# Recommendation tower, one core: a later place for layer 1, split index load at the head, low halves from copies in PSUM

## What is computed

```python
e = jnp.stack([tbl_0[ids[:, 0]], ..., tbl_25[ids[:, 25]]], axis=1)
combined = jnp.concatenate([e, r_dense_x[:, None, :]], axis=1)
z = jnp.einsum('bfd,bgd->bfg', combined, combined)[:, TRIU_I, TRIU_J]
h = jnp.concatenate([z, r_dense_x], axis=1)
h = jnp.maximum(h @ W_top1 + b_top1, 0.0)    # 479 x 512
h = jnp.maximum(h @ W_top2 + b_top2, 0.0)    # 512 x 256
y = h @ W_top3                               # 256 x 1
```

## Time and profile before

| what | value |
|---|---|
| time, median of 3 runs | 375.76 us (374.6 to 376.51) |
| profiled execution | 375.79 us, of it 373.8 us span |
| PE busy | 333.4 us (89%) |
| POOL busy | 252.8 us (68%), 256 gathers |
| DVE busy | 247.8 us (66%) |
| ACT busy | 203.4 us (54%) |
| granted TensorE clock, mean | 0.977 of 2.4 GHz |

### The profile page before, as it was taken

The page is one execution under the profiler, slowest core; times in us unless marked ns, Lnnn a source line. Parts: engine busy times, 40 slices in busy tenths (PEclk is TensorE's granted clock), DMA queues, the critical chain, the costliest instruction groups (busy, mean ns, idle before and its releaser), DMA issues.

```text
span 373.8 us, 9779 instructions
## 1 busy us (share of the span) xinstructions
PE 333.4 (89%) x4178; PEld 315.3 (84%) x4178; DVE 247.8 (66%) x298; ACT 203.4 (54%) x274; POOL 252.8 (68%) x262
## 2 busy tenths in 40 slices
PE   0768759969999899989999999989998999989967
PEld 0768649869899898989899998989898989988955
DVE  3999805994469835895389735995389645980324
ACT  1575475425756448536755456645855466548322
POOL 3888777877777777777777777777777777760000
PEclk9998979989999999999999999999999999999989
DMA  7995324453154532563254623563255524420310
GB/s 238 392 322 166 97 59 132 107 156 84 51 131 121 162 81 69 155 184 85 53 155 100 175 63 91 143 180 80 56 155 147 136 51 119 113 72 2 87 39 0
DMA packets 32377, 44.92 MB, mean 120 GB/s; under 512 B 18791, under 2 KB 20463, under 8 KB 32334
## 3 DMA queue, kind: packets, MB, share of 16 engines
q1 hardware_dynamic: 23080, 25.82, 24.0%
q0 software_dynamic: 8192, 16.79, 17.6%
q10 hardware_dynamic: 1062, 1.69, 1.4%
HBM read 38.07 MB, written 6.20 MB: 118 GB/s over the span
## 4 chain that ended last, share of the span: by engine, by line
PE 49%; DVE 21%; POOL 10%; issue 8%; DMA 6%; SPq 3%; ACT 2%; ACTq 0%; DVEq 0%
DVE hot L689 18%; PE ps_gram L458 14%; POOL emb L402 10%; PE ps_mix L476 10%; PE ps_feat L440 7%; PE ps_feat L441 7%; PE ps_feat L426 4%; PE ps_mix L510 3%; DMA products_dram<-gram 3%; SPq L329 3%; ACT feat L588 1%; DMA idx<-in_ids 1%; PE ps_mix L515 1%; PE ps_feat L476 1%; PE ps_mix L525 1%
## 5 line engine op out<-in xcount | busy, mean ns | idle before, releaser
L402 POOL DMA_INDIRECT emb<-in_tbl,idx x256 | 252.1, 985 | 81.7 <-issue 76.8
L689 DVE TENSOR_TENSOR hot<-ids_row,ps_rows 128x1024 fp32r<-128x1024 int32 x160 | 186.2, 1215 | 19.1 <-PE ps_feat L441 16.1
L440 PE MATMUL ps_feat<-hot,held_h 128*128 128x256 f32 x640 | 164.8, 295 | 15.5 <-DVE held_l L675 11.7
L588 ACT COPY feat<-ps_feat 128x512 f32<-128x512 f32 x104 | 125.7, 1229 | 76.6 <-PE ps_feat L426 44.5
L441 PE MATMUL ps_feat<-hot,held_l 128*128 128x256 f32 x640 | 159.6, 287 | 0.0
L440 PEld LDWEIGHTS ps_feat<-hot,held_h 128*128 128x128 f32 x640 | 125.0, 195 | 17.8 <-issue 14.8
L441 PEld LDWEIGHTS ps_feat<-hot,held_l 128*128 128x128 f32 x640 | 125.2, 196 | 0.0
L458 PEld LDWEIGHTS ps_gram<-feat 128*54 128x54 f32 x2048 | 56.0, 132 | 9.7 <-issue 5.4
L458 PE MATMUL ps_gram<-feat 128*54 128x54 f32 x2048 | 61.0, 217 | 1.3 <-ACT feat L588 1.3
L426 PE MATMUL ps_feat<-ident,emb 128*128 128x128 f32 x256 | 40.8, 283 | 9.0 <-DMA emb<-in_tbl,idx 9.0
L603 ACT COPY gram<-ps_gram 119x432 f32<-119x432 f32 x64 | 35.2, 550 | 9.6 <-PE ps_gram L458 9.5
(11 more groups left out here) (101 smaller groups left out, 248.4 us busy)
## 6 DMA issues: line engine op xcount, KB each, us to landing
ids_row<-in_ids_h SPq DMA_DIRECT2D x40, 256.0 KB, 3.9
products_dram<-gram SPq DMA_DIRECT2D x30, 189.0 KB
held_raw<-in_held SPq DMA_DIRECT2D x8, 512.0 KB, 13.1
emb<-in_tbl,idx POOLq DMA_INDIRECT x256
z_raw<-products_dram SPq DMA_DIRECT2D x84, 26.0 KB
held_raw<-in_held ACTq DMA_DIRECT2D x2, 512.0 KB, 9.2
dense<-in_dense_t SPq DMA_DIRECT2D x8, 128.0 KB
w1z_raw<-in_W_top SPq DMA_DIRECT2D x3, 234.0 KB
```

The lines of the kernel that those rows point to most:

```text
L402: pool.indirect_dma_start(emb[:, h, f, :], None, table, bass.IndirectOffsetOnAxis(ap=idx[:, i * UNIT + h, f:f + 1].bitcast(u32), axis=0),) ...
L440: nc.tensor.matmul(dst, held_h[:, o, c, :], hot[:, n % 2, c, :], start=c == 0, stop=False)
L588: nc.scalar.copy(feat_v[:, f, b], src).then_inc(act_out, 1)
L689: nc.vector.tensor_tensor(hot[:, n % 2, chunks, :], bass.AP(ids_row, (n % SLOTS) * UC, [[SLOTS * UC, HR], [0, PC], [1, UC]]), row_nums[:, ...
```

## The change

Five things change.

In middle units the span of the four layer 1 blocks begins at 0.74 of the list's first part, not 0.62. Below are DVE's rows from a middle unit, first before; `z_l` is the low half of a chunk, `hot` a one-hot (here of tables 8 and 9), `h_x` a rectified block, `h_l` its low half.

```diff
@@ -84,21 +85,21 @@
-    HELD_BACK = [("l1", n) for n in range(1, N1)] + [("l2", n) for n in range(N2)]
+    HELD_BACK = [("l1", n) for n in range(N1)] + [("l2", n) for n in range(N2)]
...
-        l1 = [("l1", n) for n in range(1 if last else N1)] if later else []
+        l1 = [("l1", n) for n in range(N1)] if later and not last else []
...
-                           (l1, 0.9 if last else 0.62, 1)):
+                           (l1, 0.74, 1)):
...
+        ps_raw = [banks[0:HR, :, :].rearrange("p n d -> p (n d)") for banks in (ps_mix, ps_gram)]
...
+            sp.dma_start(idx[:, 0:UNIT, :], ids_g[:, 0:UNIT, :]).then_inc(first_ids_in, 16)
             load_ids_rows(0, 0)
+
+            sp.wait_ge(held_in[0], 16)
             for o in range(AHEAD, NH):
                 if o % PER_ROW == 0:
                     load_ids_rows(0, o // PER_ROW)
                 load_table(sp, o)
+                if o == AHEAD:
+                    sp.dma_start(idx[:, UNIT:, :], ids_g[:, UNIT:, :]).then_inc(other_ids_in, 16)
...
-            pool.wait_ge(ids_in, 16)
-            for i in range(UNITS):
+            pool.wait_ge(first_ids_in, 16)
+            gather(0)
+            pool.wait_ge(other_ids_in, 16)
+            for i in range(1, UNITS):
                 gather(i)
...
+                    if i == 0:
+                        pe.wait_ge(held_split, NH)
...
-            for n in range(N1):
-                for c in range(ZC):
-                    if n == 0:
-                        pe.wait_ge(z_low, j * ZC + c + 1)
+            for c in range(ZC):
+                pe.wait_ge(z_low, j * ZC + c + 1)
+                for n in range(N1):
                     l1_chunk(j, n, c + 1)
...
+            def table_raw(o):
+
+                if o - 2 >= DIRECT:
+                    act.wait_ge(held_split, o - 1)
+                act.wait_ge(held_in[o], 16)
+                nc.scalar.copy(ps_raw[o % 2], held_raw[:, o, :, :].rearrange("p c d -> p (c d)")).then_inc(raw_copied, 1)
...
                         table_high(k[0] + 1)
+                        table_raw(k[0] + 1)
...
-            act.dma_start(idx[:], ids_g[:, :, :]).then_inc(ids_in, 16)
...
                 dve.wait_ge(held_high, o + 1)
...
+                if o < DIRECT:
...
+                else:
+                    dve.wait_ge(raw_copied, o - DIRECT + 1)
+                    nc.vector.tensor_tensor(held_l[:, o, :, :].rearrange("p c d -> p (c d)"), ps_raw[o % 2],
+                                            held_h[:, o, :, :].rearrange("p c d -> p (c d)").bitcast(fp32),
+                                            ALU.subtract).then_inc(held_split, 1)
```

More of the change, by code:

```diff
@@ L72, in dlrm_tower_kernel @@
     AHEAD = 2
+    DIRECT = 2
     BANKS = [(f, min(4, NG - f)) for f in range(0, NG, 4)]
@@ L208, in dlrm_tower_kernel @@
         ps_rows = ps("ps_rows", [128, 1, BANK])
+        ps_raw = [banks[0:HR, :, :].rearrange("p n d -> p (n d)") for banks in (ps_mix, ps_gram)]
         row_nums = ps_rows[0:HR, 0, 0:HC].bitcast(i32)
-        ids_in = sem("ids_in")
+        first_ids_in = sem("first_ids_in")
+        other_ids_in = sem("other_ids_in")
         rows_in = [[sem(f"rows_in{h}_{w}") for w in range(NB)] for h in range(UNIT)]
@@ L222, in dlrm_tower_kernel @@
         held_split = sem("held_split")
+        raw_copied = sem("raw_copied")
         w_high = sem("w_high")
@@ L639, in unit @@
                         table_high(k[0] + 1)
-            act.dma_start(idx[:], ids_g[:, :, :]).then_inc(ids_in, 16)
+                        table_raw(k[0] + 1)
             for o in range(AHEAD):
                 load_table(act, o)
-            act.wait_ge(cleared, 2)
+            act.wait_ge(cleared, 3)
             nc.scalar.copy(h1_x[:, 1, 0:1], ones[:])
@@ L647, in _ @@
                 table_high(o)
+                if o >= DIRECT:
+                    table_raw(o)
             unit(0)
@@ L674, in table_low @@
                 dve.wait_ge(held_high, o + 1)
-                nc.vector.tensor_tensor(held_l[:, o, :, :], held_raw[:, o, :, :], held_h[:, o, :, :].bitcast(fp32),
-                                        ALU.subtract).then_inc(held_split, 1)
+                if o < DIRECT:
+                    nc.vector.tensor_tensor(held_l[:, o, :, :], held_raw[:, o, :, :], held_h[:, o, :, :].bitcast(fp32),
+                                            ALU.subtract).then_inc(held_split, 1)
[3 more added lines that the diff above has]
+                                            held_h[:, o, :, :].rearrange("p c d -> p (c d)").bitcast(fp32),
+                                            ALU.subtract).then_inc(held_split, 1)
             def weights_low(n):
```

## The result

The changed kernel takes **365.19 us** (median of four runs, 364.36 to 369.97), the kernel before 376.13 us (374.6 to 377.27) in the same comparison: ratio 0.9722, 95% interval 0.9682 to 0.9762. The ratio leaves the run of 369.97 out, since it lies over 1.5% above the fastest; the median of the other three is 364.7. The profiled execution took 365.69 us, 363.9 of it span: 9.9 less span than before. It lies in the forecast range (358.6 to 366.2); the point (361.6) is 3.6 us too low, so **a quarter of the forecast gain is missing**.

The account below looks back on a forecast made before the run. PE bounds a middle unit, POOL 1.4 us behind. PE's path would gain 14.2 us to the last bank, but POOL caps it at 12.5; with -1.7 in the tail, 375.8 - 14.2 = 361.6 us, range 358.6 to 366.2.

Parts of the forecast that it names:

- Middle units, -1.0 each: Later layer 1 blocks remove PE's wait for z_l: -1.0 us per unit, 5 units, -5.0.
- It just fits: Middle units: block 2's bank is free at 253.4, PE comes to block 2 at 253.5, so no new wait.
- rival 5: Slower: rectification behind both one-hots is late in every unit, block 2 waits 3.3 us; 381.3 us, chance 0.03.
- Unit 0, -5.6: Last one-hots end 2.5 us earlier, PE's 2.60 stand for a gather goes, 0.5 of half speed goes.
- rival 3: Head: the small index load is slow and lands no earlier, POOL starts at 5.42; 363.2 us, chance 0.15.
- POOL decides: Last bank: POOL's last gather allows its transpose at 329.8, PE's path 328.1; gain up to there 12.5 us.
- Last unit, -1.0: A layer 1 block leaves ACT's path (0.75 us stood, 0.47 worked); part returns as a wait for table 9's copy.
- Tail, -1.7: Behind the last bank: chunks outside leave 12 matmuls behind the last chunk; layer 2's first half at 368.3, not 370.07.
- 0 if the clock falls: The tail's worse end: no gain if the clock falls to the 1.2 GHz level after PE has stood.
- Rival 1: Unit 0 does not shrink: rows2's gathers still land at 29.5 or a raw copy costs 1.5; 363.8 us, chance 0.2.
- signs of being wrong: Raw copies over 1.5 us, middle-unit PE wait for h_h, 1.2 GHz behind last z_l, no gather wait at the end.
- Rival 2: The PSUM operand leaves gathers slow; POOL gains only its start, 1.6 us; 367.2 us, chance 0.05.

Follow-up runs that it names:

- run 1: Changed kernel with DVE's first rectification back ahead of table 9's one-hots in units 1 to 6, PE's order left alone: 364.36 us.
- run 12: Changed kernel with the held tables' first ids (ids_row) issued ahead of the small index load on SP's queue: 370.68 us.
- run 4: Changed kernel with the old head: whole index load first on ACT's queue, SP not waiting for table 0: 367.05 us.
- run 10: Changed kernel with block 0 of layer 1 of unit 6 done again inside the last unit, at 0.9 of its list: 365.8 us.
- run 2: Changed kernel with 18 unused matmuls on PE ahead of the wait for the last unit's first chunk z: 365.36 us.
- run 3: Changed kernel with all low halves made from the raw table in SBUF again, no raw copies on ACT: 367.02 us.
- run 6: Changed kernel with the last unit's layer 1 block by block again (blocks outside, chunks inside): 368.38 us.
- run 7: Changed kernel with the edits of run 1 and run 2, plus raw PSUM copies for tables 0 and 1 too: 361.32 us.
- run 11: run 7 with weights' casts earlier on ACT, weights' low halves from PSUM copies, and 6 unused matmuls instead of 18: 357.62 us.
- run 8: The changed kernel itself measured again, without an edit: 365.9 us.

## Why the prediction was right in sign and short in size

- **Middle units, -1.0 each: 0.64.** The step that failed is "It just fits", and the fault is a reading: the prediction lets block 0 reach PE at "247.41 - 1.02 + 2.35 = 248.74", but 247.41 - 1.02 is the end of block 0's third matmul. The block itself starts at 245.87, three dense matmuls earlier, and these move with it. Redone from there, block 0 comes at 245.87 + 2.35 = 248.22 and block 2 at 248.22 + 2.84 + 1.91 = 252.97, 0.4 us before the bank is free at 253.4, and not 0.1 behind it. That is what happened: block 0 started 0.25 us behind DVE's first one-hot (117.16 and 116.91), where the prediction had 0.80 and the redone sum has 0.28, and PE stood 0.38 us. All the durations in that sum came out. The size of the gain was read too small as well: a stand of PE costs 0.27 more than its idle time, so the wait for z_l was worth 1.29 (run 1) and the new wait 0.65, and 1.29 - 0.65 is the 0.64 measured. The weak point had been named as what would be wrong ("a new PE wait for ACT's h_h in middle units") and as a mechanism in rival 5, with too high a price. In units 2 to 6 the term misses 1.8 us, in unit 1 0.5.
- **Unit 0, -5.6: 4.97, by another way.** Raw copies at 1.0, gathers freed, the stand of 2.60 gone: all as forecast. The first split came 1.5 earlier and not 2.8, since ids_row let the first one-hot start at 6.43 and not at 5.09 as before, and table 2 landed at 11.2; the last split came 1.7 earlier (37.56 against 39.25), not 2.5. Why ids_row came later stays open: its place in the queue is not the reason (run 12), and with the old head in run 4 the first one-hot started at 6.08 too. That the first gather counts for PE itself, by rows0, was not in the sum (runs 4 and 12).
- **Head: first gather 3.8 forecast, 4.21 measured**; rival 3 did not come. The Trainium skill, "DMA: Bandwidth & Descriptors", section Specifications, wants pieces of 512 B for full rate; here 16 KB in pieces of 128 B landed in 3.2 us and the 128 KB in 1 KB pieces before in 4.41. That does not test the piece's size by itself, as the bytes differ too; issued second, the same 16 KB took 5.42 (run 12).
- **"POOL decides": wrong by 2.2 us, the other way.** PE's path to the last bank gained 10.9 and not 14.2, so POOL kept slack. Of the 3.3 that PE missed, the forecast had taken 1.7 off again as POOL's floor. The floor itself was right: forecast landing 329.7, measured 329.3, and run 1 ran into it at once. Some of that is luck: the first gather came 0.4 later than forecast, and the slow gathers lost 4.1 us and not 4.9.
- **Last unit, -1.0: 0.68**, a term of the right sign that was 0.3 too large; run 10 gives 0.71 back.
- **Tail, -1.7: +1.04**, outside the ends given (-2.3 to 0), and the largest single miss: 2.7. With 3.3 - 1.7 from PE's path that is 4.3, against 365.7 - 361.6 = 4.1 of the profiled execution. Two things: the stores landed 6.04 us after issue and not 4.87, and PE then stood 2.18 us for chunk 0 and the clock fell, which costs 1.4 to 1.6 (run 2). The mechanism "0 if the clock falls" was there, its chance was not in the point. Before, the clock had fallen there as well, so most of the forecast 1.7 was the clock's return: with 1.17 for the landing taken out, the changed end with its fallen clock is 0.1 shorter than that of before. Where neither happened (runs 3 and 4) the end is 1.8 to 1.9 shorter than before, about as forecast; but run 6 gives no sign that it is the order of the loops that did this.
- **Rivals.** Rival 1's time (PE's own path is the bound, gain 10.3, 363.8) is the nearest, though not its reason: unit 0 did shrink, and the prediction does not work its 10.3 out. The range held because its upper end joins this rival to a fallen clock in the tail. Three of the four signs of being wrong that the prediction names came (the wait for h_h, 1.2 GHz behind the last z_l, no wait for gathers at the end), and the chances add up to 1.00, which left none for two misses at once. Rival 2 is refuted by runs 3 and 7, rival 5 by the middle units.

What stays open: why the last stores land in 4.9 to 5.0 us in some executions and in 6.0 in others (5.6 to 5.9 from store to loads in five of the profiles, 6.2 in one, 6.7 in the other eight, with no edit that goes with it), and what the order of the loops is worth.

## To carry to other kernels

Work out when a moved block arrives from its own first row, not from the end of a wait inside it, and read what a stand costs from start to start. When two sums that must fit lie within a few tenths of a microsecond, price the wait on both sides; a wait that is moved comes back as another, and only an edit on the engine that is late (here DVE's order, not PE's) removes it. Before counting what a bound engine gains, work out the second engine's floor (here POOL's 256 issues): it caps all that follows (run 1) until it is lifted too (runs 7 and 11). At a head, try the order of the smallest loads: here the one that started the longest chain had to go first (run 12).

## What the runs showed of the chip

- A gather beside a DVE instruction that reads two SBUF tensors takes 1.3 us (halves of the weights, 128x512, 0.69 us long) to 1.84 us (tables, 128x1024, 1.22 us) instead of 0.94; with one of them in PSUM it takes 0.94 (runs 7 and 11). The Trainium skill, "SBUF — State Buffer", section Who interferes with whom, says that a DVE instruction with two SBUF inputs contends with a GpSimd instruction that reads SBUF; the traces agree, and moving one input to PSUM is the way out.
- A copy of 128x1024 floats on ACT from SBUF to PSUM takes 1.01 us, the cast of the same tile from SBUF to SBUF 1.04.
- With the same two stands of PE (1.50 and 1.53 us) the granted clock stayed at 1.00 in one execution and fell to 0.53 in the next (run 8); at the end it fell after single stands of 2.12 to 2.97 us, and in run 6 after 0.94 and 1.79, and stayed up where 18 unused matmuls filled the stand (run 2).
